# Second attention: GpSimd makes four more of the low halves of the context rows

## The reference

```python
def _L1_xattn_ref(input_1, input_2, Wq, bq, Wk, bk, Wv, bv):
    ...
    Q = jnp.einsum('bld,de->ble', input_1, Wq) + bq
    K = jnp.einsum('bld,de->ble', input_2, Wk) + bk
    V = jnp.einsum('bld,de->ble', input_2, Wv) + bv
    scores = jnp.einsum('bqd,bkd->bqk', Q, K) * scale
    scores = jnp.clip(scores, -100.0, 100.0)
    weights = jax.nn.softmax(scores, axis=-1)
    return jnp.einsum('bqk,bkd->bqd', weights, V)
```

## Time and profile before

| | |
|---|---|
| median of 3 runs | 1176.95 us |
| lowest, highest | 1174.17, 1177.15 us |
| the profiled execution's own time | 1175.05 us |
| its span | 1173.3 us |
| around the span | 1.75 us |
| mean granted TensorE clock | 1.000 |
| busy: TensorE, VectorE, ScalarE, GpSimd | 97%, 76%, 77%, 50% of the span |

### The profile page before, as it was taken

How to read it: one execution, slowest core, us unless ns; L and a number is a source line. 1 busy time by engine, 2 the same in 40 slices (tenths; PEclk the granted TensorE clock), 3 DMA queues, 4 the chain that set the end, 5 groups by cost and what they waited for, 6 DMA issues and landing times.

```text
span 1173.3 us, 32542 instructions
## 1 busy us (share of the span) xinstructions
PE 1138.9 (97%) x12748; PEld 814.0 (69%) x12749; DVE 889.1 (76%) x1718; ACT 901.3 (77%) x1552; POOL 583.9 (50%) x548
## 2 busy tenths in 40 slices
PE   8999999999999999999999999999997899889998
PEld 6566666666666666666666666666666758767898
DVE  7777878888888888888878787878774659788632
ACT  5699988889988889898888888889884278586010
POOL 5355656565655565665656565656564070043000
PEclk9999999999999999999999999999999999999999
DMA  5465544445354545354545454544443995150385
GB/s 223 107 183 149 153 116 119 127 95 154 90 154 96 150 92 157 90 154 95 148 95 142 107 138 110 137 108 93 123 92 97 382 341 167 33 180 1 109 285 176
DMA packets 141142, 163.31 MB, mean 139 GB/s; under 512 B 18320, under 2 KB 127280, under 8 KB 140992
## 3 DMA queue, kind: packets, MB, share of 16 engines
q1 hardware_dynamic: 139904, 157.20, 48.0%
q10 hardware_dynamic: 1088, 4.06, 0.9%
HBM read 71.60 MB, written 12.99 MB: 72 GB/s over the span
## 4 chain that ended last, share of the span: by engine, by line
PE 85%; DVE 6%; ACT 4%; issue 2%; DMA 1%; SPq 1%; POOL 0%; DVEq 0%; ACTq 0%; POOLq 0%
PE ps L900 21%; PE ps L872 21%; PE ps L938 7%; PE ps L914 7%; PE ps L2353 4%; PE ps L957 4%; PE ps L955 4%; PE ps L956 4%; PE ps L1681 3%; PE ps L2361 2%; PE ps L1108 2%; ACT ss_decay L1936 2%; PE ps L2135 1%; DMA k_st<-k_rest 1%; PE ps L2117 1%
## 5 line engine op out<-in xcount | busy, mean ns | idle before, releaser
L468 POOL TENSOR_TENSOR pT_lo<-p_exp,pT_hi 128x896 f16<-128x896 f32 x223 | 420.8, 1887 | 313.9 <-ACT pT_hi L580 313.9
L561 ACT ACTIVATE p_exp<-ps,ln_k,esc 128x896 f32<-128x896 f32 x224 | 246.0, 1098 | 54.7 <-PE ps L938 47.1
L693 DVE TENSOR_REDUCE tile_max<-ps 128x128 f16<-128x896 f32 x224 | 244.4, 1091 | 49.6 <-PE ps L914 47.2
L580 ACT ACTIVATE pT_hi<-p_exp 128x896 f16<-128x896 f32 x224 | 211.8, 946 | 1.0
L688 DVE TENSOR_TENSOR v_lo<-ps,v_hi 128x512 f16<-128x512 f32 x196 | 135.4, 691 | 68.6 <-ACT v_hi L553 66.2
L956 PE MATMUL ps<-v_lo,pT_hi 128*128 128x64 f16 x1568 | 164.4, 193 | 0.0
L955 PE MATMUL ps<-v_hi,pT_hi 128*128 128x65 f16 x1568 | 164.3, 193 | 0.1
L957 PE MATMUL ps<-v_hi,pT_lo 128*128 128x65 f16 x1568 | 163.8, 193 | 0.0
L900 PE MATMUL ps<-c_hi,wk_hi 128*128 128x448 f16 x448 | 158.5, 354 | 0.8 <-DVE k_rest L708 0.5
L900 PE MATMUL ps<-c_hi,wk_lo 128*128 128x448 f16 x448 | 157.9, 352 | 0.0
L900 PE MATMUL ps<-c_lo,wk_hi 128*128 128x448 f16 x448 | 157.8, 352 | 0.0
(11 more groups left out here) (406 smaller groups left out, 2074.8 us busy)
## 6 DMA issues: line engine op xcount, KB each, us to landing
k_st<-k_top SPq DMA_DIRECT2D x444, 112.0 KB, 2.3
k_st<-k_rest SPq DMA_DIRECT2D x444, 56.0 KB, 2.0
xa_cn<-in_ctx SPq DMA_DIRECT2D x14, 896.0 KB, 7.5
me_w<-in_me_w SPq DMA_DIRECT2D x8, 1536.0 KB, 6.3
c_raw<-in_ctxT SPq DMA_DIRECT2D x13, 896.0 KB, 5.6
ctx_parts<-c_hi SPq DMA_DIRECT2D x14, 448.0 KB, 3.3
ctx_parts<-c_lo SPq DMA_DIRECT2D x14, 448.0 KB, 2.8
me_w<-in_me_w SPq DMA_DIRECT2D x8, 768.0 KB, 5.9
```

The lines of the kernel that those rows point to most:

```text
L468: nc.gpsimd.tensor_tensor(pT_lo[:, n % 2, :, :].rearrange("p t s -> p (t s)"), p_exp[:, n % 2, :], pT_hi[:, n % 2, :, :].rearrange("p t s ...
L561: nc.scalar.activation(p_exp[:, n % 2, :], s_scores[n % 2], ACT.Exp, bias=ln_k[:, 0:1], scale=esc[:, n // H0 % 2:n // H0 % 2 + 1]).then_in ...
L580: nc.scalar.activation(pT_hi[:, n % 2, :, :].rearrange("p t s -> p (t s)"), p_exp[:, n % 2, :], ACT.Copy).then_inc(pT_hi_ready, 1)
L693: nc.vector.tensor_reduce(tile_max[:, n % 2, :], s_scores[n % 2].rearrange("p (t s) -> p s t", s=S), AX.X, ALU.max).then_inc(tile_max_done, 1)
```

## The change

The twelve early halves on GpSimd become sixteen: k = 12 to 15, the four halves of chunks 6 and 7, move from VectorE to GpSimd. VectorE's loop still counts them in their places and makes nothing there. ScalarE leaves these rows unscaled, as before, so GpSimd needs two instructions for each: it multiplies the rows in place by the scale, a column repeated over 896, and subtracts the high half. The two are linked. `wait_low` takes the marks of GpSimd for k < 16.

```diff
+POOL_HALVES = EARLY_HALVES + 4
...
         def wait_low(engine, k):
-            if k < EARLY_HALVES:
+            if k < POOL_HALVES:
                 engine.wait_ge(plink.sem, low_marks[k])
             else:
-                engine.wait_ge(E["cn_lo_ready"], k - EARLY_HALVES + 1)
+                engine.wait_ge(E["cn_lo_ready"], k - POOL_HALVES + 1)
...
-            for k in range(EARLY_HALVES):
+            for k in range(POOL_HALVES):
                 c, b = k // 2, k % 2
+                raw = half(cn, c % RING, b)
                 pool.wait_ge(E["cn_hi_ready"], k + 1)
-                link(nc.gpsimd.tensor_tensor(half(cn_lo, c, b), half(cn, c % RING, b), half(cn_hi, c, b), ALU.subtract))
+                if k >= EARLY_HALVES:
+                    link(nc.gpsimd.tensor_tensor(raw, raw, nat[:, 0:1].to_broadcast([P, CH]), ALU.mult))
+                link(nc.gpsimd.tensor_tensor(half(cn_lo, c % SLOTS, b), raw, half(cn_hi, c % SLOTS, b), ALU.subtract))
                 low_marks.append(link.count)
...
                 for _ in range(LATE_HALVES.get(c, 0)):
-                    slot = k // 2 % SLOTS
-                    v.wait_ge(E["cn_hi_ready"], k + 1)
-                    nc.vector.scalar_tensor_tensor(...)
+                    if k >= POOL_HALVES:
+                        slot = k // 2 % SLOTS
+                        v.wait_ge(E["cn_hi_ready"], k + 1)
+                        nc.vector.scalar_tensor_tensor(...)
                     k += 1
```

More of the change, by code:

```diff
@@ L1639, in _ @@
                 for _ in range(LATE_HALVES.get(c, 0)):
-                    slot = k // 2 % SLOTS
-                    v.wait_ge(E["cn_hi_ready"], k + 1)
-                    nc.vector.scalar_tensor_tensor(out=half(cn_lo, slot, k % 2), in0=half(cn, k // 2 % RING, k % 2), scalar=nat[:, 0:1],
-                                                   in1=half(cn_hi, slot, k % 2), op0=ALU.mult, op1=ALU.subtract).then_inc(E["cn_lo_ready"], 1)
+                    if k >= POOL_HALVES:
+                        slot = k // 2 % SLOTS
+                        v.wait_ge(E["cn_hi_ready"], k + 1)
+                        nc.vector.scalar_tensor_tensor(out=half(cn_lo, slot, k % 2), in0=half(cn, k // 2 % RING, k % 2), scalar=nat[:, 0:1],
+                                                       in1=half(cn_hi, slot, k % 2), op0=ALU.mult, op1=ALU.subtract).then_inc(E["cn_lo_ready"], 1)
                     k += 1
```

## The result

| | before | changed |
|---|---|---|
| median, timed together | 1175.13 us (6 runs, 1173.94 to 1177.15) | 1180.32 us (6 runs, 1179.69 to 1181.37) |
| the profiled execution's own time | 1175.05 us | 1180.18 us |
| its span | 1173.3 us | 1178.4 us |

The ratio is 1.0044, with a 95% interval of 1.0034 to 1.0054: slower by 5.2 us, clear of the 0.3% bound. The span grew by 5.1 us.

What follows compares the result with a forecast made beforehand. TensorE, idle only 1.86 us in the stretch, left little to win; a late load of chunk 10 would stall ScalarE and delay chunk 9 by 4.9 us: 1176.95 + 4.9 = 1181.9 us, range 1177.5 to 1184.0.

Steps and rivals of the forecast that it cites:

- What bounds: Second half of second cross-attention: TensorE idles 1.86 of 44.00 us, the most a quicker VectorE could win.
- GpSimd's price: Each half on GpSimd: multiply 1.68 us, subtraction 1.89, 3.73 with links, where VectorE needed 1.06.
- The exclusion: GpSimd and VectorE instructions with two SBUF operands exclude each other entirely, making k = 15 8.0 us later; chance 0.67.
- The near tie: VectorE's k = 18 (989.75) against GpSimd's subtraction of k = 15 (989.8); VectorE was taken to go first.
- that order: GpSimd's subtraction of k = 15 goes before VectorE's k = 18, done at 991.7: +4.0 us, within the exclusion's 0.67.
- the sum: Delay of chunk 9's weighing: +4.9 us with GpSimd and VectorE excluding each other, +2.5 us without.
- From the landing on: After chunk 10's rows land at 997.7, 7.3 us to weighing chunk 9 at 1005.0; later loads wanted later.
- Behind chunk 9: After chunk 9's weighing nothing is won back; VectorE's chain to the end is the old one, shifted.
- The base: Time of the kernel before to which the loss was added: 1176.95 us, 1.9 above the profiled execution.

Runs made afterwards that it cites:

- The late load alone: Kernel before, with SyncE's load of chunk 10 waiting for k = 19 instead of k = 15; stretch +5.08 us, ratio 1.0048.
- The run with one-column remainders: Changed kernel with VectorE's remainders k = 16 to 19 made over one column only; stretch +2.94 us, ratio 1.0018.
- three halves at better places: Against the kernel before, only late halves k = 18, 22 and 27 on GpSimd, k = 12 to 15 on VectorE; -1.18 us to the transposes of `u`, ratio 0.9990.
- the run that also moved the bias: Late halves k = 18, 22 and 27 on GpSimd, VectorE adding the value bias to x behind chunk 1, not 12; 1173.43 us, ratio 0.9983 against before.

## Why the prediction was right

- **What bounds.** Right: TensorE idled 1.86 us in the stretch, no run here won clearly more than that, and ScalarE's order of time, not VectorE's, held the answer. The late load alone gives +5.08 us.
- **GpSimd's price.** The multiply was put at 1.68 us from two rows of other widths; it is 1682 ns. k = 13 was done on time, and the load of chunk 9 (out at 982.6) cost nothing, as said.
- **The exclusion**, read off one instruction of the first attention, carried over to another width and another stage. Step by step: GpSimd's third subtraction, 984.37 to 987.00, was to end at 987.2; k = 15 was to be done at 992.6 and is at 992.4, in a profile that runs 0.28 us ahead. The near tie of VectorE's k = 18 (989.75 against 989.8) fell as taken, with 0.04 us between them; that was luck. With leads of 0.02 and 0.03 us for VectorE in the record, GpSimd went first (k = 21 above, and the one-column k = 17 below), and the prediction's own price for that order is +4.0 instead of +4.9. The Trainium skill's rule ("GPSIMD Engine Reference", Specifications, on two SBUF inputs of VectorE) gave the kind of collision; the rows gave its form and price. The run with one-column remainders splits the loss nearly as the sum had: 2.9 us without the exclusion (forecast 2.5) and 2.5 with what it leaves out (forecast 2.4 for the exclusion).
- **From the landing on.** 7.3 us were counted from ScalarE's k = 20 to the weighing of chunk 9; it is 7.61 (997.61 to 1005.22). The step that was off is "The loads of chunks 11 and 12 pass behind chunk 10's ... and are wanted later than it". Chunk 11's is wanted 3.6 us later (k = 22 at 1001.18 against k = 20 at 997.61), but issued 0.5 us behind chunk 10's, it took 8.8 us to land, 4.2 behind it, with the DMA engines full in between (share 1.09, 351 GB/s, from 997.5 to 1001.7; chunk 10's load of before, by itself: 0.63, 186), and held ScalarE up by 0.46. VectorE's k = 22 then waited for ScalarE, and its two remainders took 2.44 us instead of 2.21:

```profile
1001.43 2.44 DVE L1647 SCALAR_TENSOR_TENSOR xa_cn_lo<-xa_cn,nat,xa_cn_hi 128x896 f16<-128x896 f32 x2
```

  That makes 0.2 of the 0.5 us between +4.9 and +5.44 in the stretch. Another 0.2 is ScalarE's start of k = 20, 997.89 in the old trace's time (997.61 and the 0.28) where 997.7 was forecast, and 0.1 is spread over the way to chunk 9.
- **Behind chunk 9** nothing was lost or won: 13.11 against 13.12 us.
- **The number.** 1181.9 was forecast, 1180.32 measured. The base is what was off: I added to the median of three runs, 1176.95, which with three more is 1175.13. The base was 1.8 us too high and the loss added to it 0.3 too low against the timed 5.2, so the two misses cancelled in small part. Added to the profiled execution's own time the sum was 1179.95, and that execution of the changed kernel took 1180.18.

## What to carry to other kernels

Before handing work to an idle engine, list who waits for the result, the queue that reloads its input buffer among them, and take the earliest of them, with the transfer's time added, as the due time: here it was 1.5 us where TensorE's own was far off. An idle engine that takes 3.7 us for what another does in 1.06 can be free for two halves and cost 5 us for four. And choose the pieces by where the busy engine is late, not by number: three halves at better places won 1.2 us (2.0 in the run that also moved the bias), where four at the first places lost 5.

## What the runs showed that I had not expected

**The turn is taken even for one column.** In the run with one-column remainders, VectorE's k = 17, one element wide, began 0.03 us ahead of GpSimd's multiply of 986.96 in the record, right behind its subtraction of 984.98:

```profile
986.93 1.72 DVE L1648 SCALAR_TENSOR_TENSOR xa_cn_lo<-xa_cn,nat,xa_cn_hi 128x1 f16<-128x1 f32 x1
988.57 0.54 DVE L1630 CAST xa_pT<-ps 128x384 f16<-128x384 f32 x1
```

It took 1.72 us, until 988.65, where the multiply ended at 988.64, and held up the cast behind it. Its k = 16, one element wide too, ran from 984.19 to 984.92, where GpSimd's multiply of 983.22 ended at 984.90. So in this run a narrow VectorE instruction waited for GpSimd like a wide one, and GpSimd hardly waited for it. (Between two of VectorE's own such instructions GpSimd got its turn: k = 19 waited, above.)

**TensorE's clock.** In the change TensorE stood for 2.67 us and the granted clock stayed at 1.00, the upper of its levels, 2.4 GHz. In the old kernel with the late load it stood for 3.67 us, and by stretch of time the clock was this (window, its length, busy time of TensorE, its weight loads, VectorE, ScalarE and GpSimd, then the granted clock, DMA share, GB/s):

```profile
990.00:998.00 8.00, 4.64 (x41) 3.80 (x39) 3.30 (x6) 1.97 (x3) 0.00 (x0) 0.95 0.71 223
998.00:999.50 1.50, 0.97 (x5) 0.98 (x6) 1.45 (x3) 1.50 (x4) 0.00 (x0) 0.50 1.06 343
...
1001.00:1003.00 2.00, 2.00 (x11) 1.45 (x10) 1.95 (x4) 2.00 (x5) 0.00 (x0) 0.50 0.19 60
1003.00:1006.00 3.00, 3.00 (x25) 2.52 (x24) 2.82 (x5) 2.92 (x5) 0.00 (x0) 0.82 0.84 274
1006.00:1010.00 4.00, 4.00 (x39) 3.67 (x37) 3.97 (x6) 3.97 (x7) 0.00 (x0) 1.00 0.01 2
```

It fell to 0.50, 1.2 GHz, during the wait, which began at 994.86: by half microseconds it was 1.00 until 997.0, 0.50 from 997.5 to 1004.0, and back at 1.00 from 1004.5. From the first weighing of chunk 8 to the next transposes TensorE needed 4.26 us (1000.08 to 1004.34) instead of 2.29, and this is why chunk 9 was 6.18 us late. Most of it did not last, because VectorE sets the end of the stretch, and VectorE lost little: its cast behind the remainder k = 23 came 1.29 us behind the start of that remainder, 0.24 later than in the change (1005.46 to 1006.51).

```profile
1004.01 1.14 DVE L1642 SCALAR_TENSOR_TENSOR xa_cn_lo<-xa_cn,nat,xa_cn_hi 128x896 f16<-128x896 f32 x1
1005.30 0.56 DVE L1626 CAST xa_pT<-ps 128x384 f16<-128x384 f32 x1
```

So the clock's share in the +5.08 us is about 0.2. The rest of the comparison with the change adds up: reckoned from the first weighing, ScalarE had the load 0.45 us earlier (25.74 against 26.19 us), VectorE's two remainders waited 0.14 less for the load of chunk 11 (2.30 against 2.44), and the stretch is 0.36 us shorter. The forecast costed TensorE's standing still at nothing; that held in the change's trace, where it stood for 2.67 us; in the other run, where it stood for 3.67, the clock fell.
